# Attention over 2048 keys: value weighting issued whole, two key tiles behind, between the second and third pair of matmuls

## The reference

```python
# first layer ("L0_attn"): 16 heads of 16 channels, every token attends to all 2048
def _L0_attn_ref(x, Wq, bq, Wk, bk, Wv, bv, Wo, bo):
    q = _rope(proj(Wq, bq)); k = _rope(proj(Wk, bk)); v = proj(Wv, bv)
    scores = jnp.einsum('bhtd,bhsd->bhts', q, k) / scale        # scale = sqrt(16)
    attn = jax.nn.softmax(scores, axis=-1)
    out = jnp.einsum('bhts,bhsd->bhtd', attn, v)
    return jnp.einsum('btc,oc->bto', out, Wo) + bo
# second layer ("L0_ffn"), twice: windowed attention with 8 heads of 64 channels and
# a window of 128, then layernorm, w1, gelu gate, w2
x = x + _layernorm(_L0_attn_ref(_layernorm(x), ...))
x = x + _layernorm(_L0_ffn_ref(_layernorm(x), ...))
```

## Time and profile before

| | us |
|---|---|
| median of 3 runs | 2990.77 (2990.61 to 2994.27) |
| the profiled execution | 2994.74 |
| span of its trace | 2992.9 |
| first attention, first score to last weighting (window 229.10 to 1579.60) | 1350.50 |

### The profile page before, as it was taken

The page is one execution under the profiler, slowest core; times in us unless marked ns, Lnnn a source line. Parts: engine busy times, 40 slices in busy tenths (PEclk is TensorE's granted clock), DMA queues, the critical chain, the costliest instruction groups (busy, mean ns, idle before and its releaser), DMA issues. The chain is left out here.

```text
span 2992.9 us, 61908 instructions
## 1 busy us (share of the span) xinstructions
PE 2828.6 (95%) x23360; PEld 1770.2 (59%) x23360; DVE 2425.0 (81%) x4390; ACT 2263.6 (76%) x4928; POOL 1133.7 (38%) x1617
## 2 busy tenths in 40 slices
PE   8969999999999999999998599999999899999996
PEld 5733333333333333333335488888888788888885
DVE  5668999999999999999945577777777688888884
ACT  4407888888888888888887477777777678788883
POOL 4510000000000000000005476667666667777774
PEclk9958999999999999999999799999999999999998
DMA  4332343323343343324315000000001100000000
GB/s 131 124 77 47 55 68 60 64 52 63 60 67 54 57 68 60 60 53 65 60 20 180 20 4 5 5 5 4 5 5 61 63 10 19 19 15 19 19 19 29
DMA packets 74524, 140.12 MB, mean 47 GB/s; under 512 B 21760, under 2 KB 43712, under 8 KB 67520
## 3 DMA queue, kind: packets, MB, share of 16 engines
q1 hardware_dynamic: 69696, 134.88, 21.6%
q10 hardware_dynamic: 4544, 1.38, 0.2%
HBM read 88.63 MB, written 43.38 MB: 44 GB/s over the span
## 5 line engine op out<-in xcount | busy, mean ns | idle before, releaser
L646 DVE TENSOR_REDUCE mx<-aux 128x1 f32<-128x1024 f32 x1024 | 1250.3, 1224 | 83.6 <-PE aux L515 72.0
L616 ACT ACTIVATE probs<-scores 128x512 f32<-128x512 f32 x2048 | 1117.9, 597 | 221.9 <-PE scores L539 108.6
L515 PE MATMUL aux<-k_stack,q_stack 48*128 48x512 f32 x2048 | 777.2, 458 | 31.6 <-DMA k_stack<-qk_dram 23.2
L539 PE MATMUL scores<-q_stack,k_stack 50*128 50x512 f32 x2048 | 767.1, 450 | 0.8 <-DMA q_stack<-rows_dram 0.7
L551 PE MATMUL pv<-probs,v_ones 128*32 128x256 f32 x8192 | 656.8, 392 | 0.1
L539 PEld LDWEIGHTS scores<-q_stack,k_stack 50*128 50x128 f32 x2048 | 312.4, 185 | 412.5 <-ACT probs L616 390.3
L483 POOL CAST w_raw_hi<-w_raw 128x576 fp32r<-128x576 f32 x30 | 20.0, 667 | 1179.2 <-DMA w_raw<-in_ff_weights 1179.2
L551 PEld LDWEIGHTS pv<-probs,v_ones 128*32 128x32 f32 x8192 | 161.5, 108 | 366.4 <-ACT probs L616 286.0
L515 PEld LDWEIGHTS aux<-k_stack,q_stack 48*128 48x128 f32 x2048 | 314.5, 190 | 87.4 <-DVE mx L646 51.8
L1337 ACT ACTIVATE probs<-probs,negmax 128x256 f32<-128x256 f32 (+1 forms) x512 | 250.0, 490 | 69.5 <-DVE negmax L1412 69.5
L1136 POOL TENSOR_TENSOR rnorm<-norm_min,minus_half 128x8 f32<-128x8 f32 x128 | 234.2, 1830 | 10.7
(11 more groups left out here) (184 smaller groups left out, 5551.1 us busy)
## 6 DMA issues: line engine op xcount, KB each, us to landing
q_stack<-qk_dram SPq DMA_DIRECT2D x192, 128.0 KB, 5.0
k_stack<-qk_dram SPq DMA_DIRECT2D x192, 128.0 KB, 6.8
w_raw<-in_ff_weights SPq DMA_DIRECT2D x30, 288.0 KB, 9.3
split_dram<-w_raw_hi SPq DMA_DIRECT2D x30, 288.0 KB, 2.1
split_dram<-w_raw_lo SPq DMA_DIRECT2D x30, 288.0 KB, 2.4
qk_dram<-qkT_hi SPq DMA_DIRECT2D x32, 256.0 KB, 3.1
qk_dram<-qkT_lo SPq DMA_DIRECT2D x32, 256.0 KB, 3.6
x_ring<-x_dram SPq DMA_DIRECT2D x32, 128.0 KB, 3.6
```

The lines of the kernel that those rows point to most:

```text
L515: last = nc.tensor.matmul(aux[:, ring["unit"], block_of_keys % 2], q_stack[rows, r % BODY, tile * P:(tile + 1) * P], k_stack[rows, r % BOD ...
L539: nc.tensor.matmul(scores[:, item % BANKS1], k_stack[0:SCORE_ROWS, r % BODY, s * P:(s + 1) * P], q_stack[0:SCORE_ROWS, r % BODY, j * 512:( ...
L616: nc.scalar.activation(probs[:, item % PROBS], scores[:, item % BANKS1], ACT.Exp, scale=float(D1) ** -0.5).then_inc(probs_ready, 1)
L646: nc.vector.reduce_max(mx[:, slot, tile, half:half + 1], aux[:, unit].rearrange("p a k -> p (a k)"), AX.X).then_inc(max_taken, 1)
```

## The change

It replaces the halves of the weighting by one whole of 512 columns. It is issued for the tile two steps back in all cases, after slot 1, that is between the second and the third of the four pairs of matmuls of a step. The two transposes of a head leave `aux`, and take a bank in the ring of three that the scores use. ACT copies both out of it, and POOL in the place of DVE divides the output by the sum. The two maximum rows go from SBUF to SBUF without DRAM. DVE combines a head's maxima behind the first reduction of the next head. ACT copies `pv` three slots later. SP's and POOL's loops over heads are written out. `UNITS`, `BANKS1`, `AHEAD` and the place of the score pairs stay as they are.

```diff
@@ PE: the maxima
-                if block_of_keys % 2 == 0:
-                    ring["unit"] = ring_unit()
+                unit, half = divmod(BLOCKS * (TB * r + tile) + block_of_keys, 2)
+                if half == 0 and unit >= UNITS:
+                    pe.wait_ge(max_taken, unit - UNITS + 1)
...
@@ PE: weighting
-            def weigh(r, s, half):
+            def weigh(r, s):
...
-                pe.wait_ge(probs_ready, BLOCKS * (TB * r + s + 1))
-                columns = slice(half * HALF, (half + 1) * HALF)
+                pe.wait_ge(scores_freed, number["exp", r, s, BLOCKS - 1] + 1)
                 for j in range(BLOCKS):
-                    last = nc.tensor.matmul(pv[VW * j:VW * (j + 1), columns], v_ones[:, r % BODY, s, :], probs[:, (BLOCKS * (TB * r + s) + j) % PROBS, columns],
-                                            start=(s == 0 and half == 0), stop=(s == TB - 1 and half == 1), skip_group_check=True, tile_position=(0, VW * j))
-                if half == 1:
-                    last.then_inc(pv_done, 1)
+                    last = nc.tensor.matmul(pv[VW * j:VW * (j + 1)], v_ones[:, r % BODY, s, :], probs[:, (BLOCKS * (TB * r + s) + j) % PROBS],
+                                            start=(s == 0), stop=(s == TB - 1), skip_group_check=True, tile_position=(0, VW * j))
+                last.then_inc(pv_done, 1)
...
@@ PE: the order of a step
-                    if j == 0:
-                        weigh_earlier(r, d, s, 2, 1, left, first)
-                    if j == (3 if s == 1 else 2):
-                        weigh_earlier(r, d, s, 1, 0, left, first)
+                    if j == 1:
+                        weigh_two_back(r, d, s, left, first)
                     if j == 2 and (d, s) == (0, ROWS_STEP) and left >= 1:
                         maximum_rows(r + 1)
                     if j == 2 and (d, s) == (1, OUT_STEP) and not first:
                         output_item(r)
...
@@ PE: the ring of three banks, with both transposes in it
+            def begin(item):
+                if number[item] >= BANKS1:
+                    pe.wait_ge(scores_freed, number[item] - BANKS1 + 1)
+                return scores[:, number[item] % BANKS1]
...
-                unit = ring_unit()
-                nc.tensor.transpose(aux[:, unit, 0, 0:P], m_parts[:], ident[:]).then_inc(rows_in_psum, 1)
+                nc.tensor.transpose(begin(("rows", r))[:, 0:P], m_parts[:], ident[:]).then_inc(scores_ready, 1)
...
@@ SP: the two rows
-                sp.dma_start(rows_dram[n].rearrange("a (t c) -> (a t) c", c=P), m_rows[:].bitcast(F32)).then_inc(rows_stored, 16)
-                sp.wait_ge(rows_stored, 16 * (r + 1))
-                sp.dma_start(q_stack[SPLIT_ROWS:SCORE_ROWS, slot, :].bitcast(F32), rows_dram[n]).then_inc(rows_loaded[slot], 16)
+                for part in range(2):
+                    row = q_stack[SPLIT_ROWS + part:SPLIT_ROWS + part + 1, slot, :].rearrange("a (t c) -> a t c", c=P)
+                    sp.dma_start(row.bitcast(F32), m_rows[part * TB:(part + 1) * TB].bitcast(F32)).then_inc(rows_loaded[slot], 16)
...
@@ POOL: the output, behind split_max_and_v of each head; local_mask stays behind the last head
+            def write_output(n):
+                pool.wait_ge(scores_freed, number["out", n] + 1)
+                nc.gpsimd.tensor_tensor(out=rsum[:], in0=o_raw[:, :, :, D1], in1=minus_ones[:], op=ALU.pow).then_inc(rsum_made, 1)
+                pool.wait_ge(rsum_made, n + 1)
+                nc.gpsimd.tensor_tensor(out=QO[:, n].rearrange("p (j c) d -> p c j d", j=4), in0=o_raw[:, :, :, 0:D1],
+                                        in1=rsum[:].unsqueeze(3).to_broadcast([P, 4, 4, D1]), op=ALU.mult).then_inc(o_made, 1)
...
@@ ACT
+            def copy_output(n):
+                src = take(("out", n))
+                if n:
+                    act.wait_ge(o_made, n)
+                nc.scalar.copy(o_raw[:], src.rearrange("p (c j d) -> p c j d", c=4, j=4)[:, :, :, 0:D1 + 1]).then_inc(scores_freed, 1)
...
-                        if (d, s, j) == (1, 1, 1):
+                        if (d, s, j) == (1, 2, 0):
                             act.wait_ge(pv_done, TB * (n + 1))
                             nc.scalar.copy(o_stage[:], pv[:]).then_inc(pv_copied, 1)
...
@@ DVE: reductions alone, and the maxima of a head one reduction later
-                if (tile, half) == (TB - 1, 1):
-                    dve.drain().then_inc(maxima_written, 1)
...
-                nc.vector.reciprocal(rsum[:, n % BODY].rearrange("p (c j) -> p c j", c=4), item[:, :, :, D1]).then_inc(rsum_made, 1)
...
+            for unit in range(2 * TB * NH):
+                n, tile, half = unit // (2 * TB), unit // 2 % TB, unit % 2
+                dve.wait_ge(max_in_psum, unit + 1)
+                nc.vector.reduce_max(mx[:, n % BODY, tile, half:half + 1], aux[:, unit % UNITS].rearrange("p a k -> p (a k)"), AX.X).then_inc(max_taken, 1)
+                if n and unit % (2 * TB) == 0:
+                    head_maximum(n - 1)
+            head_maximum(NH - 1)
```

More of the change, by code:

```diff
@@ L382, in max_item, with heads, bank_items @@
             return d + a, local // BLOCKS, local % BLOCKS
[L384 to L395, removed]
-            return items
[L398 to L418, removed]
+        FIRST_ROWS = TB * 2 + 4
+        def heads():
+            return [(n, min(NH - 1 - n, 2)) for n in range(NH)]
+        def bank_items():
+            items = [("rows", 0)] + [("exp", 0, s, j) for s in range(LEAD) for j in range(BLOCKS)]
+            for n, left in heads():
+                for d, s in steps():
+                    for j in range(BLOCKS):
+                        if left >= d:
+                            items.append(("exp", n + d, s, j))
+                        if j == 2 and (d, s) == (0, ROWS_STEP) and left >= 1:
+                            items.append(("rows", n + 1))
+                        if j == 2 and (d, s) == (1, OUT_STEP):
+                            items.append(("out", n))
+            return items
+        number = {item: at for at, item in enumerate(bank_items())}
         @block.sync
@@ L588, in step @@
                         output_item(r)
-            def head(n, left):
-                for d, s in steps():
-                    step(n, d, s, left)
             for m in range(AHEAD):
@@ L599, in _, with take @@
                 step(-1, 1, s, 2, first=True)
-            assert ring["item"] == PROLOGUE_ITEMS + 1
-            written_out_heads(head)
+            for n, left in heads():
+                for d, s in steps():
+                    step(n, d, s, left)
         @block.scalar
         def _(act):
-            def copy_rows(r, unit):
-                act.wait_ge(rows_in_psum, r + 1)
-                nc.scalar.copy(m_rows[:], aux[0:2 * TB, unit, 0, 0:P]).then_inc(rows_copied, 1)
-                act.drain().then_inc(rows_freed, 1)
+            def take(item):
+                act.wait_ge(scores_ready, number[item] + 1)
+                return scores[:, number[item] % BANKS1]
@@ L613, in exponentiate @@
-                act.wait_ge(scores_ready, item + 1)
-                if j == 0 and item >= PROBS:
+                src = take(("exp", r, s, j))
+                at = BLOCKS * (TB * r + s) + j
+                if j == 0 and at >= PROBS:
                     act.wait_ge(pv_done, TB * r + s - PROBS // BLOCKS + 1)
-                nc.scalar.activation(probs[:, item % PROBS], scores[:, item % BANKS1], ACT.Exp, scale=float(D1) ** -0.5).then_inc(probs_ready, 1)
-            def head(r, left):
-                for d, s in steps():
-                    for j in range(BLOCKS):
-                        if (d, s, j) == (1, 1, 1):
-                            act.wait_ge(pv_done, TB * (r + 1))
-                            nc.scalar.copy(o_stage[:], pv[:]).then_inc(pv_copied, 1)
-                        if (d, s, j) == (0, ROWS_STEP, 3) and left >= 1:
-                            place = [what[3] for what in aux_items(left)].index("rows")
-                            copy_rows(r + 1, (first_unit(left) + place) % UNITS)
-                        if left >= d:
-                            exponentiate(r + d, s, j)
@@ L664, in head @@
-            def head(n, left):
-                for at, (d, s, j, kind, what) in enumerate(aux_items(left)):
-                    unit = (first_unit(left) + at) % UNITS
-                    if kind == "max":
-                        take_max((n + what[0]) % BODY, what[1], what[2], unit)
-                    if kind == "out":
-                        write_output(n, unit)
-            units = [("max", u) for u in range((AHEAD + BLOCKS * LEAD) // 2)]
-            units.insert(FIRST_ROWS, ("rows", 0))
```

159 lines of the change are left out of this document (66 added, 93 removed).

## The result

The changed kernel takes 3321.14 us (median of 4 runs, 3311.61 to 3338.28), the kernel before 2992.52 beside it (2990.61 to 3001.08): ratio 1.1077, 95% interval 1.1034 to 1.1121. The forecast was 3314 us and a ratio of 1.108. The profiled execution took 3338.28 us, the longest of the four.

The account below looks back on a forecast made before the run. The PE's own order was taken as the pace, 2.47 us a step. Steps +318.4, start −1.3 and tail +6.3 gave +323.4 on the profiled 2994.7, so 3318.1, less 4.0 to the runs' median: 3314 us, range 3275 to 3370, 86%.

Parts of the forecast that it names:

- step: claim, maximum, weighting, slot 2, reduction: Chain holding a unit of `aux` through the weighting; it becomes the step, 3.28 us against 2.47, bounds 3.06 and 3.41.
- head in the middle: Two combinings of maxima 52.4 us apart in mid-stage; the 2.8 us a head of late items vanish in the wait.
- step at the lower clock: Early steps up to 246.1 us at granted 0.50: about 2.8 steps of 4.7 us each, 4.1 us more.
- last steps without maxima: The 20.75 steps after the maxima run out, bound by the banks of scores: 2.65 us each, 55.0 us.
- the 512 steps: All steps of the attention stage together: 1668.9 us against 1350.5, +318.4.
- tail: Behind the last head: two whole weightings +1.2, POOL's division +3.8, the mask on POOL +1.3; in all +6.3 us.
- start: First score comes 1.3 us earlier, because the first maximum rows no longer take a unit.
- The length of the whole weighting: Start of a 512-column weighting to the next pair on the PE: 1.01 us, bounds 0.79 and 1.14.
- What costs nothing: Transposes, DMAs, ACT's copies, combining of maxima and POOL's division hide in the PE's 0.8 us standing or DVE's 0.9 idle.
- That the wait isn't there: Rival: the unit is free in time and the PE's own 2.33 us is the step; about 2839 us; 4%.
- The banks as the pace: Rival: the three banks of scores set the step, 2.65 us; 3002 us, no change; 2%.
- The clock falls: Rival: the PE's standing each step lowers its clock; about 3990 us throughout, 3650 for half the steps; 7%.

Follow-up runs that it names:

- the narrow weighting: Changed kernel with the weighting of 14 of a head's 16 key tiles on 256 of 512 columns; 3604.85 us, ratio 1.2007.
- weighting after slot 0: Changed kernel with the whole weighting issued after slot 0, between two items of maxima, not after slot 1; 3080.4 us, ratio 1.0236.
- 84 ahead: Changed kernel with the maxima 84 slots ahead and not 83, so the weighting stands between two items; 3038.85 us, ratio 1.0106.
- claim behind: Changed kernel with the maximum of slot 1 issued behind the weighting, its score still before it; 3045.18 us, ratio 1.0139.
- the two with short reductions: Reductions over 512 of 1024 scores: in the changed kernel, 3075.36 us; in the kernel before with half weightings after slots 1 and 3, 3006.19 us.
- the kernel before with the order alone: Kernel before with only the weighting changed: whole, two tiles back, after slot 1; 3383.0 us, ratio 1.1235.
- halves inside both items: Kernel before with its two half weightings one slot later, after slots 1 and 3; 3334.25 us, ratio 1.1076.

## Why the prediction was right

The mechanism was read from one place a head in the trace of before, and it is what happened in every step.

| term | predicted | measured |
|---|---|---|
| step: claim, maximum, weighting, slot 2, reduction | 0.05 + 0.43 + 1.01 + 0.57 + 1.22 = 3.28 | 0.06 + 0.42 + 1.00 + 0.57 + 1.22 = 3.27 |
| head in the middle | 52.4, nothing late | 52.4 |
| step at the lower clock | 4.7, about 2.8 of them | 4.73, about 8 (up to 289.0 us) |
| last steps without maxima | 2.65 | 2.61 |
| the 512 steps | +318.4 | +322.9 |
| tail | +6.3 | +4.7 (the power 2.90 us and not 3.4; the last two weightings +0.1 and not +1.2) |
| start | −1.3 | −1.0, beside 17.6 us of the projections that are not the change's |

The steps came out 4.5 us longer in all. The lower clock lasted for about 5 steps more than forecast, at 1.45 us each some 7 us, and the step of 3.27 and not 3.28 gives part of it back. No term is off by more than 8 us, so the total is not a lucky sum of large misses.

*The length of the whole weighting* was the term with the widest bounds, 0.79 to 1.14. The prediction took two rows of the same instruction at the two clocks and split it into a part that goes with the columns and one that doesn't. That gave the length to 0.01 us (1.00 measured), and the narrow weighting bears it out (0.43 for half of the columns).

*What costs nothing* held, and so did the order in which things come: the score of slot 1 starts 1.19 us after slot 2 (forecast 1.2, by its bank), its maximum 1.85 after it (1.84). All that the change adds once a head went into the PE's standing. It held only because of that standing, as the kernels without it show (43.9 and 43.1 us a head for a step of 2.61, where 41.8 would be the bare sum).

*One reading is off, and nothing hangs on it:* from 786.00 to 786.28 it is 0.28 us; the 0.23 that the prediction names is the stretch up to the end of the reduction at 786.23.

*The rivals.* That the wait isn't there: all five kernels that shorten the chain or take it apart (weighting after slot 0, 84 ahead, claim behind, and the two with short reductions) move as the chain says. The banks as the pace: it is the next one, 2.61 us, with the weighting after slot 0 and with the maxima 84 ahead, and not in the changed kernel. (With the claim behind the weighting the step is 2.62, which the PE's own 2.66 would give as well, so that kernel doesn't tell the two apart.) In these kernels the step came as given, but not the total: with the chain gone it was to reach the time of before, and it stayed 1.1 to 2.4% above it, by what comes late once a head, and after slot 0 also by the 23 us of lower clock at the end. *The clock falls* (7%): it didn't, save that it rose later (289.0 us). The runs don't support that this was as safe as 7% says: two kernels with the same kind of wait lost the clock. The Trainium skill (TensorE: Matmul & The Clock Gate, "A second HAM failure mode: psum-queue depth-cycling") tells of a kernel whose PE idles briefly and often between its groups of matmuls, and whose clock swings between its two levels. The traces of those two kernels agree with it (0.90 and 0.55 granted), and that of the changed kernel, with 0.8 us of standing in each step and 1.00 granted, does not. The edit between it and the narrow weighting is the width of 14 of 16 weightings and nothing else. Why the clock fell in the one and stayed up in the other, and how far the changed kernel was from losing it, was not measured.

What stays open: why the last steps without maxima ran at the lower clock with the weighting after slot 0 and in the kernel before with the order alone, and not in the changed kernel, with the same PE instructions in nearly the same order.

## What to carry to other kernels

Where a buffer of PSUM is filled by several matmuls, whatever the PE does between the first and the last of them is time in which the buffer is held and can't yet be read. Put long work between items, not into one, and count the loop claim, fill, read, release as one sum against the step. If a hand-written order has one place that is out of the pattern, read it first: it shows what the rest would cost in that pattern. And an engine that is busy for only 70% of such a loop (DVE, 1136 of 1569 us) still sets the pace, since each of its instructions is a link.

## What the runs showed of the hardware that was not expected

Less work on the PE made the kernel slower. With the full weighting, the PE standing some 0.8 us of 3.27 (by the starts; the profile, which models the ends of matmuls, shows 0.38 idle), the granted clock was 1.00 from 289.0 us to the end of the heads. With a weighting of half the columns and the same chain it was 0.55 (about 1.2 GHz for most of the time), and with halves inside both items 0.90. With those same halves and a shorter reduction, where the PE hardly waits, it was 1.00 again. A table of busy times doesn't show such a loss: with the narrow weighting PE was busy 396.58 of 400 us, at 0.55.
